# A dense and graph network in one kernel: the second feed-forward layer with stationary weights, and the end of the kernel in two halves of the nodes

## The reference

```python
# layer 2: feed-forward with a capacity (once per image, 4096 positions)
weights = (x @ wr + br)[..., 0]
_, idx = jax.lax.top_k(weights, S // 2)        # 2047 of them are used
y = gelu(sel @ w1 + b1) @ w2 + b2              # 128 -> 512 -> 128
processed = zeros_like(x).at[idx].set(y * weights[idx])
x = x + processed + x_normed

# layer 4: experts, gated by a graph attention over 524288 edges and self loops
agg = segment_softmax_sum(edges) + b_gat       # 16 values for each of 16384 nodes used
scores = layernorm(agg).reshape(M, 4, 4).mean(1)
w = softmax(top_k(scores, 2))
out = sum(g_e * (gelu(x @ W1[e] + b1[e]) @ W2[e] + b2[e]) for e in range(4))
x = x + x_normed_part + out
```

## Time and profile before

| | |
|---|---|
| median of 3 runs | 7333.31 us (7291.48 to 7333.96) |
| the profiled execution | 7323.2 us, of which the core's span is 7321.3 us |
| busy PE, PEld | 3180.6 us (43%), 1979.4 us (27%) |
| busy DVE, ACT, POOL | 3408.2 us (47%), 1543.3 us (21%), 2635.4 us (36%) |
| chain that ended last | PE 27%, another core or an unknown queue 23%, DVE 18%, issue 16% |

### The profile page before, as it was taken

One profiled execution on the slowest core, in us unless ns is written; L12 is line 12 of the kernel. 1 busy time (PEld: TensorE's weight loads), 2 busy tenths in 40 slices (PEclk: granted clock), 3 DMA queues, 4 the chain that ended last, 5 costly groups with the idle time before them and its releaser, 6 DMA issues.

```text
span 7321.3 us, 84797 instructions
## 1 busy us (share of the span) xinstructions
PE 3180.6 (43%) x32140; PEld 1979.4 (27%) x32141; DVE 3408.2 (47%) x6941; ACT 1543.3 (21%) x3954; POOL 2635.4 (36%) x2472
## 2 busy tenths in 40 slices
PE   0011157687997798778873122222222222222204
PEld 0011146543773485256622000000000000000104
DVE  9999965567767685845674111111111111111128
ACT  0000034321751373045410011111111111111100
POOL 0000013210000000023003777777777777777450
PEclk9965578786997798678875555655655655655657
DMA  2000040001000100010003222222222222222207
GB/s 79 0 0 0 0 167 13 22 11 29 12 2 1 38 4 1 0 28 3 2 0 42 27 32 32 32 32 32 32 32 32 32 32 32 32 32 32 63 7 247
DMA packets 259708, 227.82 MB, mean 31 GB/s; under 512 B 115005, under 2 KB 222954, under 8 KB 250282
## 3 DMA queue, kind: packets, MB, share of 16 engines
q0 software_dynamic: 78944, 29.28, 6.4%
q1 hardware_dynamic: 99786, 99.91, 4.4%
...
## 4 chain that ended last, share of the span: by engine, by line
PE 27%; another core or an unknown queue 23%; DVE 18%; issue 16%; DVEq 7%; ACT 4%; DMA 3%; POOL 2%; ACTq 1%; SPq 0%; POOLq 0%
DVE SA_ L1308 3%; PE PSB L1160 3%; PE PSB L382 3%; DVE SA_ L1298 2%; PE PSB L527 2%; PE PSB L366 2%; PE PSB L679 2%; POOL VPAD L961 2%; DVE SA_ L583 2%; PE PSB L352 1%; DVEq L1389 1%; PE PSB L392 1%; PE PSB L661 1%; DMA VPAD<-s_TNT 1%
## 5 line engine op out<-in xcount | busy, mean ns | idle before, releaser
L951 POOL DMA_INDIRECT SA_<-s_T,GIX x2048 | 2192.7, 1071 | 657.8 <-issue 657.8
L1160 PE MATMUL PSB<-VPAD,EH 128*128 128x512 f32 x512 | 303.0, 756 | 1996.2 <-DMA VPAD<-s_TNT 1819.6
L943 POOL DMA_INDIRECT s_AEXP<-fill,SIX x128 | 141.3, 1104 | 2331.9 <-DMA fill<-s_ADT 2122.7
L899 DVE TENSOR_TENSOR XPAD<-SA_ 128x256 f32<-128x256 f32 x32 | 14.2, 443 | 1833.9 <-DMA SA_<-s_T,GIX 1779.5
L1160 PEld LDWEIGHTS PSB<-VPAD,EH 128*128 128x128 f32 x512 | 122.1, 247 | 2199.0 <-DMA VPAD<-s_TNT 1863.3
L850 POOL DMA_INDIRECT SA_<-s_SK,BLKI x128 | 146.0, 1140 | 1251.8 <-DVE BLKI L1441 978.7
L1164 PE MATMUL PSB<-SA_,EW 128*128 128x512 f32 x512 | 346.7, 826 | 345.4 <-ACT SA_ L1145 233.1
L303 ACT ACTIVATE PRX<-PSB,MX 128x144 f32<-128x144 f32 x1024 | 375.3, 379 | 417.0 <-DVE MX L224 414.2
L1412 PE MATMUL PSB<-ident,SA_ 128*128 128x128 f32 x448 | 83.3, 369 | 837.2 <-DVE SA_ L1379 575.3
L1149 ACT ACTIVATE VPAD<-PSB,PRX 128x512 f32<-128x512 f32 x128 | 87.9, 687 | 1308.3 <-remote 918.5
L1145 ACT ACTIVATE SA_<-PSB,PRX 128x512 f32<-128x512 f32 x256 | 175.9, 687 | 777.3 <-remote 431.5
...
## 6 DMA issues: line engine op xcount, KB each, us to landing
SA_<-s_T,GIX POOLq DMA_INDIRECT x2048
...
```

The costliest lines, as they stand in the source:

```text
L951: pool.indirect_dma_start(out=n.G[:,s,c,:],out_offset=None,in_=d["T"],in_offset=IOA(ap=n.GIX[s][:,c:c+1],axis=0)).then_inc(n.gath[s],16)
L1160: pe.matmul(PSB[:,(m%4)*512:(m%4+1)*512],n.WM1[:,m//2,(m%2)*P:(m%2+1)*P],n.TNC[:,s,:],start=True,stop=True).then_inc(n.moe_h,1)
```

## The change

**Feed-forward.** The second layer now has `W2` stationary and 512 columns of `HTL` moving: 4 matmuls for a group, result with channels on partitions. The bias is added by ACT from a column, `B2C`. When the loop over the groups is over, PE turns each group back with four transposes into PSUM bank 0 or 1, and DVE takes the gated sums from PSUM. New semaphores: `s_gs` (DVE has read the last count, bank 1 is free), `s_yt` (a group is turned), `s_yg` (its sums are done).

**Tail.** Gathers, node arithmetic and mix are cut into two halves of 64 tiles. The gathers are issued as before, on two semaphores. DVE and ACT go node half 0, mix of chunks 0 to 15, node half 1, mix of chunks 16 to 31. Temporaries of the halves are apart. PE's and SP's mix loops are unchanged.

```diff
@@ l0ffn_dve
-    dve.tensor_tensor(n.PFX[:,:],n.PFX[:,:],cnt[:,64:96],ALU.add); dve.drain()
+    dve.tensor_tensor(n.PFX[:,:],n.PFX[:,:],cnt[:,64:96],ALU.add); dve.drain().then_inc(n.s_gs,1)
...
     for g in range(8):
         if g: dve.drain(); Ln.stats(dve,n,range(4*g-4,4*g))
-        dve.wait_ge(n.s_ya,b*8+(g+1))
-        for t in range(4*g,4*g+4):
-            dve.scalar_tensor_tensor(out=n.X[:,t,:],in0=n.Y[:,t,:],scalar=n.GS[:,t:t+1],in1=n.X[:,t,:],op0=ALU.mult,op1=ALU.add)
+        dve.wait_ge(n.s_yt,b*8+(g+1))
+        for i in range(4):
+            t=4*g+i; o=g%2*512+i*P
+            last=dve.scalar_tensor_tensor(out=n.X[:,t,:],in0=PSB[:,o:o+P],scalar=n.GS[:,t:t+1],in1=n.X[:,t,:],op0=ALU.mult,op1=ALU.add)
+        last.then_inc(n.s_yg,1)
@@ l0ffn_act
-        act.activation(n.Y[:,4*g:4*g+4,:],PSB[:,(6+g%2)*512:(7+g%2)*512].rearrange("p (t c) -> p t c",c=C),ACT.Copy).then_inc(n.s_ya,1)
+        act.activation(n.Y[:,512*g:512*(g+1)],PSB[:,(6+g%2)*512:(7+g%2)*512],ACT.Identity,bias=n.B2C[:,0:1]).then_inc(n.s_ya,1)
@@ l0ffn_pe
-        for i in range(4):
-            o=PSB[:,(6+g%2)*512+i*P:(6+g%2)*512+(i+1)*P]
-            pe.matmul(o,ones[0:1,:],n.B2R[:,:],start=True,stop=False)
-            for m in range(4):
-                last=pe.matmul(o,n.HTL[:,g%2,m,i*P:(i+1)*P],n.W2[:,m,:],start=False,stop=(m==3))
+        for m in range(4):
+            last=pe.matmul(PSB[:,(6+g%2)*512:(7+g%2)*512],n.W2[:,m,:],n.HTL[:,g%2,m,:],start=(m==0),stop=(m==3))
         last.then_inc(n.s_y,1)
         if 2*g+2<COUNTS: count(2*g+2)
+    pe.wait_ge(n.s_gs,b+1)
+    for g in range(8):
+        pe.wait_ge(n.s_ya,b*8+(g+1))
+        if g>=2: pe.wait_ge(n.s_yg,b*8+(g-1))
+        for i in range(4):
+            o=g%2*512+i*P
+            last=pe.transpose(PSB[:,o:o+P],n.Y[:,512*g+P*i:512*g+P*(i+1)],ident)
+        last.then_inc(n.s_yt,1)
@@ edges_pool
-        pool.indirect_dma_start(out=n.RE[:,t,:],out_offset=None,in_=d["R"],in_offset=IOA(ap=n.EIX[:,t:t+1],axis=0)).then_inc(n.re_g,16)
+        pool.indirect_dma_start(out=n.RE[:,t,:],out_offset=None,in_=d["R"],in_offset=IOA(ap=n.EIX[:,t:t+1],axis=0)).then_inc(n.re_g[t//NH],16)
@@ node_dve (its instructions keep their order; NT=128 tiles become NH=64)
-def node_dve(dve,n,SA):
-    o=[4096]
+def node_dve(dve,n,SA,h):
+    o=[4096+h*HALFTMP]; part=slice(h*NH,(h+1)*NH)
...
-    dve.wait_ge(n.re_g,16*NT)
+    dve.wait_ge(n.re_g[h],16*NH)
@@ mix_dve
-    with dve.Fori(0,NCK//MIX) as i:
+    k=NCK//MIX//2
+    with dve.Fori(h*k,(h+1)*k) as i:
@@ mix_act
-    with act.Fori(0,NCK//MIX) as i:
+    with act.Fori(h*k,(h+1)*k) as i:
@@ build
-            node_dve(dve,n,m.SA)
-            mix_dve(dve,n,PSB)
+            for h in range(2): node_dve(dve,n,m.SA,h); mix_dve(dve,n,PSB,h)
...
-            node_act(act,n,m.SA)
-            mix_act(act,n,out,m.tick)
+            for h in range(2): node_act(act,n,m.SA,h); mix_act(act,n,out,m.tick,h)
```

More of the change, by code:

```diff
@@ L766 @@
 IOA=bass.IndirectOffsetOnAxis
-NCK=NODES//512; MIX=4
+NCK=NODES//512; MIX=4; NH=NODES//128//2; HALFTMP=66*NH
 def declare_nodes(nc,ctx,n,SA,m):
@@ L1070, in node_dve @@
     dr=dve.drain
[L1071 removed]
+    b1=lambda a,k: a.to_broadcast((P,NH,k))
     h4=lambda a: a.rearrange("p t (h e) -> p t h e",h=4)
[L1073 to L1076 removed]
+    be=lambda a: a.unsqueeze(3).to_broadcast((P,NH,4,4))
+    TBN,ADN,VAL,RE,G4=(x[:,part] for x in (n.TBN,n.ADN,n.VAL,n.RE,n.G4))
+    if h==0: dve.wait_ge(n.tbn_ld,16*4); dve.wait_ge(n.ad_ld,16); dve.wait_ge(n.ad_ld2,16)
+    dve.tensor_tensor(mS,TBN[:,:,16:20],ADN,ALU.add)
+    dve.tensor_scalar(VAL,VAL,-1.0,BIG,ALU.add,ALU.mult); dr()
     dve.scalar_tensor_tensor(out=mS,in0=mS,scalar=0.2,in1=mS,op0=ALU.mult,op1=ALU.max)
[L1078 to L1079 removed]
+    dve.wait_ge(n.re_g[h],16*NH)
+    dve.tensor_tensor(mE,RE[:,:,0:4],VAL.unsqueeze(2).to_broadcast((P,NH,4)),ALU.add); dr()
     dve.tensor_tensor(M,mE,mS,ALU.max); dr()
     dve.tensor_tensor(mE,mE,M,ALU.subtract)
[L1082 to L1086 removed]
+    dve.tensor_tensor(mS,mS,M,ALU.subtract).then_inc(n.nd_dve,1)
+    dve.wait_ge(n.nd_act,h*3+1)
+    dve.tensor_tensor(DEN,RE[:,:,4:8],mE,ALU.mult)
+    dve.tensor_tensor(h4(MSG),h4(RE[:,:,8:24]),be(mE),ALU.mult); dr()
+    dve.tensor_tensor(DEN,DEN,mS,ALU.add); dve.tensor_tensor(h4(T16),h4(TBN[:,:,0:16]),be(mS),ALU.mult); dr()
     dve.tensor_tensor(MSG,MSG,T16,ALU.add); dve.tensor_scalar(DEN,DEN,1e-16,None,ALU.add); dr()
@@ L1116, in node_dve @@
     first(M2,I2)
-    dve.tensor_tensor(T1,M2,M1,ALU.subtract).then_inc(n.nd3,1)
-    dve.wait_ge(n.nd3e,1)
+    dve.tensor_tensor(T1,M2,M1,ALU.subtract).then_inc(n.nd_dve,1)
+    dve.wait_ge(n.nd_act,h*3+3)
     dve.tensor_scalar(M1,T1,1.0,None,ALU.add); dr()
@@ L1122, in node_dve, with node_act @@
     dve.tensor_tensor(I1,I1,b1(M1,4),ALU.mult); dve.tensor_tensor(I2,I2,b1(M2,4),ALU.mult); dr()
-    dve.tensor_tensor(n.G4[:,:,:],I1,I2,ALU.add).then_inc(n.g_rdy,1)
+    dve.tensor_tensor(G4,I1,I2,ALU.add)
     dr()
-def node_act(act,n,SA):
-    o=4096
-    act.wait_ge(n.nd1,1)
-    act.activation(SA[:,o:o+NT*8],SA[:,o:o+NT*8],ACT.Exp).then_inc(n.nd1e,1)
-    act.wait_ge(n.nd2,1)
-    vr=o+NT*(4*4+32+4+1)
-    act.activation(SA[:,vr:vr+NT],SA[:,vr:vr+NT],ACT.Sqrt).then_inc(n.nd2e,1)
-    t1=vr+NT*(1+8+3)
-    act.wait_ge(n.nd3,1)
-    act.activation(SA[:,t1:t1+NT],SA[:,t1:t1+NT],ACT.Exp).then_inc(n.nd3e,1)
+def node_act(act,n,SA,h):
+    o=4096+h*HALFTMP
+    act.wait_ge(n.nd_dve,h*3+1)
+    act.activation(SA[:,o:o+NH*8],SA[:,o:o+NH*8],ACT.Exp).then_inc(n.nd_act,1)
+    act.wait_ge(n.nd_dve,h*3+2)
+    vr=o+NH*(4*4+32+4+1)
+    act.activation(SA[:,vr:vr+NH],SA[:,vr:vr+NH],ACT.Sqrt).then_inc(n.nd_act,1)
+    t1=vr+NH*(1+8+3)
+    act.wait_ge(n.nd_dve,h*3+3)
+    act.activation(SA[:,t1:t1+NH],SA[:,t1:t1+NH],ACT.Exp).then_inc(n.nd_act,1)
 def experts_act(act,n,PSB,d,i,s):
@@ L1199, in mix_dve, with mix_act @@
             last.then_inc(n.mix_dv,1)
-def mix_act(act,n,out,tick):
-    o=out.rearrange("(t p) c -> p t c",p=P)
-    with act.Fori(0,NCK//MIX) as i:
+def mix_act(act,n,out,tick,h):
+    o=out.rearrange("(t p) c -> p t c",p=P); k=NCK//MIX//2
+    with act.Fori(h*k,(h+1)*k) as i:
         for s in range(MIX):
@@ L1205, in mix_act @@
             act.dma_start(o[:,bass.ds((i*MIX+s)*4,4),:],n.X3C[s]).then_inc(n.mix_out[s],16)
-    for s in range(MIX): act.wait_ge(n.mix_out[s],NCK//MIX*16)
+    if h:
+        for s in range(MIX): act.wait_ge(n.mix_out[s],NCK//MIX*16)
 EDGES=524288; INVALID=NODES; NBLK=COLS//BLK; ROWBITS=12; BITS=19
```

35 lines of the change are left out of this document (12 added, 23 removed).

## The result

The changed kernel takes 7274.40 us (7259.45 to 7312.72) against 7317.97 us (7284.58 to 7341.50) for the kernel before, a ratio of 0.9947, 95% interval 0.9929 to 0.9965. The ratio is that of the means, which lie 39 us apart (the medians 44); 91 were forecast, so less than half of it came, and the kernel is within 1% of no change. The time lies 0.6 us inside the top of the stated range, 7195 to 7275, and that is luck: the range was counted from a median before of 7333, which is 7318 here. The profiled execution, 7312.72 us, is the longest of the changed kernel's 14, so it is read stage by stage and not by its end.

What follows compares the result with a forecast made beforehand. No engine was busy for half the span, so stages were read singly: PE set the feed-forward; gathers, node arithmetic and mix followed in a row in the tail. -26 and -65 us gave -91, forecast 7240 us, range 7195 to 7275.

Steps and rivals of the forecast that it cites:

- rival 2: Feed-forward: the new transposes are exposed because a PSUM bank returns too late; 58 us gained, not 91, 7275 us; chance 0.07.
- the digit round: Feed-forward: the search's rounds keep up with the shortened PE block, about 0.4 us to spare, so nothing is taken off.
- Feed-forward: Second layer with stationary weights: 20.5 us of PE saved, 13.9 added, net -6.6 us an image, -26 us over four.
- ACT's copy: Feed-forward: grows a bias but lies beside PE's work and costs nothing; without that cover, 3 us in all.
- the transposes: Feed-forward: four a group, 0.63 us at full clock, about 1.1 at half, hidden behind DVE's gated sums.
- Rival 1, the clock: New transpose phase: PE's clock falls and the next stage starts low; 14 us over four images, 7254 us; chance 0.10.
- (a): Tail: node work of half 0 starts on the 64th gather, at 7006.9 in place of 7089.54, -82.6 us.
- (b): Tail: node instructions issued twice at half length, 37.4 us each half; with preparation on the path, +15.4 us.
- (d): Tail: four mix chunks reload during node half 1, so half 1's mix starts from full buffers, -1 us.
- (c): Tail: half 0's mix runs beside the second 64 gathers, sharing DMA engines; 3 us lost, between 0 and 8.
- rival 3: Tail: second gathers starve beside mix and DVE; 7289 us if late, 7340 and more if slower; chances 0.09 and 0.03.
- The rule weighed with it: Tail: GpSimd can't write its DMA descriptors during DVE's two-port modes; most node work held exempt; no size given.

Runs made afterwards that it cites:

- e2: Only the feed-forward edits, with the tail of the kernel before, against the kernel before: 6812.8 us against 6835.1, ratio 0.9967.
- e15: The whole changed kernel, run again unchanged, against the kernel before: 6736.9 us against 6832.7, ratio 0.9855.
- 90-us sets: Sets of timings, each on one chip, where the kernel before took 7304 to 7318 us and its edge stage about 89 us a chunk of 64 gathers.
- e1: The whole changed kernel, run again unchanged, against the kernel before: 6743.3 us against 6835.1, ratio 0.9875.
- 82-us sets: Sets of timings, each on one chip, where the kernel before took 6833 to 6841 us and its edge stage about 82 us a chunk of 64 gathers.

## Why the prediction was wrong, point by point

**Its arithmetic** holds but for trifles: with 35.2 us off 91, rival 2 leaves 56 us and not 58, and the digit round has 0.55 us to spare, not 0.4.

**Feed-forward: right.** Forecast 6.6 us an image; measured 5.9, 6.4, 6.4 and 6.4. ACT's copy, the digit round (3.66 us) and the transposes are hidden as argued, and rival 2 did not come about.

**Rival 1, the clock, came in part.** Two windows of the new transpose phase, image 1 of the changed kernel:

```profile
2187.00:2192.00 5.00, 1.65 (x12) 0.99 (x10) 4.82 (x20) 1.53 (x2) 0.00 (x0) 1.00 0.01 2
2193.00:2202.00 9.00, 3.60 (x14) 2.15 (x12) 8.64 (x37) 0.00 (x0) 0.00 (x0) 0.50 0.00 0
```

The granted clock is at the 2.4 GHz level in the first and at the 1.2 GHz level in the second, after PE had gone from a full loop to a third of each 2 us. Four transposes took 0.63 us and then 1.09, and both stayed hidden. The Trainium skill, "TensorE: Matmul & The Clock Gate", Part 4: PE-mode transpose, says that the full clock does not engage for transposes; the fall here is what it would lead to expect, since the 0.63 us rows stand right behind a full loop. The set of 0.63 us at 2874.89 in this profile disagrees, as the earlier trace rows did: PE had done nothing but transposes since 2868.28, at 1.94 to 1.96 us for two sets, and the clock rose from the 1.2 to the 2.4 GHz level under them. What I priced, a slow start of the stage that follows, is not where it went: the whole third layer comes in a short form of 239 to 247 us and a long one of 250 to 253, in kernels with and without the edit. Summed over four images it is 973 us on average in five profiles without the edit (965 to 981) and 986 in fifteen with it (968 to 1001). That points to some 12 us given back through the clock, about the rival's 14, and would explain the 22 us of e2 where its feed-forwards gained 26. With ranges that overlap it is likely, not shown.

**Tail, (a), (b), (d): right.** 81.1 us to the start everywhere; 37 us a node half and 82 to 88 us a mix half in every set without the stall, and in the others for the second half.

**Tail, (c): the step that failed.** I counted what the second gathers share with the rest, DMA engines (4 us) and POOL's time, and took 3 us, 8 at most. On the POOL side that was right: the gathers stayed 1.25 us apart in the median (1.31 in the mean), and rival 3 fell. The rule weighed with it (the Trainium skill, "SBUF — State Buffer", section "SBUF: two separate sides") would have DVE hold up POOL in its two-port modes; here DVE was held up while POOL issued gathers. What I didn't count is that the *instructions* of the other engines slow down beside POOL's indirect DMAs: by 24 us in the node part and 24 in the mix. Of the forecast 65 us, 18.5 were left.

**The trace of before had shown it, in stages I didn't read.** Its second stages, images 0 to 3, in windows from L144 to L144 (columns as above):

```profile
990.26:1417.98 427.72, 333.67 (x6276) 254.99 (x6276) 220.56 (x502) 204.73 (x702) 138.20 (x120) 0.85 0.20 70
1812.81:2110.48 297.67, 261.64 (x6308) 216.40 (x6307) 222.60 (x508) 201.38 (x701) 0.00 (x0) 0.94 0.08 11
2480.51:2776.38 295.87, 260.45 (x6302) 215.13 (x6302) 222.38 (x507) 201.42 (x701) 0.00 (x0) 0.94 0.07 11
3142.05:3547.41 405.36, 328.23 (x6300) 258.81 (x6299) 223.80 (x507) 204.98 (x701) 96.06 (x96) 0.82 0.07 4
```

The same work, with 120 and 96 indirect DMAs of POOL beside it in images 0 and 3, takes 130 and 110 us longer, 1.1 us for each of them. In image 3 it isn't the data: the DMA engines are busy for 7% there as in image 2. And ACT in its edge stage, where the expert layers run beside the gathers:

```profile
4932.05 0.69 ACT L1145 ACTIVATE SA_<-PSB,PRX 128x512 f32<-128x512 f32 x1 [4.21 <-remote]
...
4942.56 0.69 ACT L1145 ACTIVATE SA_<-PSB,PRX 128x512 f32<-128x512 f32 x1 [4.23 <-issue]
4953.80 0.69 ACT L1149 ACTIVATE VPAD<-PSB,PRX 128x512 f32<-128x512 f32 x1 [10.55 <-remote]
4965.03 0.69 ACT L1149 ACTIVATE VPAD<-PSB,PRX 128x512 f32<-128x512 f32 x1 [10.54 <-remote]
```

("Remote" is another core or a queue that the profile doesn't show.) And at the same place in e15:

```profile
4665.44 0.69 ACT L1153 ACTIVATE SA_<-PSB,PRX 128x512 f32<-128x512 f32 x1 [0.17 <-PE PSB L1168]
4667.16 0.69 ACT L1157 ACTIVATE VPAD<-PSB,PRX 128x512 f32<-128x512 f32 x1 [1.03 <-PE PSB L1172]
4668.87 0.69 ACT L1157 ACTIVATE VPAD<-PSB,PRX 128x512 f32<-128x512 f32 x1 [1.03 <-PE PSB L1172]
```

Between 4200 and 6300 us ACT has over 200 gaps of more than 4 us before these lines in the two profiles of before in 90-us sets, and 26 in e1 and e15. PE's matmuls of the same loop (L1164) have 271 us of idle time before them in the profile of before, 89 of it put down to issue, and none in e15.

A rate of 1.1 us for each of 64 gathers, taken from those windows, would have put up to 70 us against the gain of the tail, and the forecast for it between nothing and 65 us; it was 47 us, 0.73 for each. But the same stages without a loss in the 82-us sets show that no trace of one chip could have told the loss on another. I read only the two stretches that the diff touches, and in those nothing lay beside the gathers: the cost of an overlap can't be seen where there is none yet.

**Open.** Shown is that DVE stalls while POOL issues gathers beside it, in the 90-us sets, and not without them. That what is slow is the fetching of instructions is inferred: waits with nothing awaited, operations of their usual length, instructions used up and not time, gaps on DVE, PE and ACT, in loops too. No row shows a fetch. Why chips differ in it, and what spacing is enough, wasn't found.
